# Causal attention on one core: softmax sums by rounded ones, clips in the bank, other order of roundings

## What is computed

```python
x = L0_attn_x                                  # (4, 512, 512), float32
xn = _layernorm(x)
x = x + _L0_attn_ref(xn, ...) + _L0_ffn_ref(xn, ...)

def _L0_attn_ref(x, W_DQ, W_UQ, W_QR, W_DKV, W_UK, W_UV, W_KR, W_O):   # 16 heads of 128, rotary part of 64
    c_Q = x @ W_DQ.T                                                   # latent of 128
    q = concat([c_Q @ W_UQ.T, rope(c_Q @ W_QR.T)])                     # per head
    c_KV = x @ W_DKV.T
    k = concat([c_KV @ W_UK.T, rope(x @ W_KR.T)])                      # rotary part shared by all heads
    v = c_KV @ W_UV.T
    scores = clip(einsum('bhqd,bhkd->bhqk', q, k), -80, 80)
    scores = where(causal, scores, -inf)
    weights = softmax(scores / sqrt(192))
    return (weights @ v, heads side by side) @ W_O.T
```

## Time and profile before

| | |
|---|---|
| median of 3 runs | 1333.8 us (1333.33 to 1334.8) |
| profiled execution | 1334.99 us, its span 1333.0 us |
| PE busy | 1304.3 us, 98% |
| DVE busy | 736.7 us, 55% |
| ACT busy | 620.4 us, 47% |
| POOL busy | 627.9 us, 47% |
| in 900 to 1000 us | PE 100.0, DVE 84.8, ACT 65.5, POOL 69.6 us |
| mean granted clock of PE | 0.996 |

### The profile page before, as it was taken

One profiled execution on the slowest core, in us unless ns is written; L12 is line 12 of the kernel. 1 busy time (PEld: TensorE's weight loads), 2 busy tenths in 40 slices (PEclk: granted clock), 3 DMA queues, 4 the chain that ended last, 5 costly groups with the idle time before them and its releaser, 6 DMA issues.

```text
span 1333.0 us, 21124 instructions
## 1 busy us (share of the span) xinstructions
PE 1304.3 (98%) x6553; PEld 1090.8 (82%) x6553; DVE 736.7 (55%) x1349; ACT 620.4 (47%) x1146; POOL 627.9 (47%) x534
## 2 busy tenths in 40 slices
PE   5999999999999999999997999999999999999999
PEld 4788888888888888888885888888888888888887
DVE  6361154332222222222224878988888888788876
ACT  6421243222222222222224766676667666766674
POOL 5125584994060005000003467666766676666543
PEclk9999999999999999999998999999999999999999
DMA  8225453664142114212115123233233332322012
GB/s 268 65 87 220 185 187 96 186 187 143 57 151 64 57 57 127 86 57 64 57 52 181 34 47 70 65 64 74 39 83 63 61 64 58 77 43 60 17 48 95
DMA packets 72952, 123.23 MB, mean 92 GB/s; under 512 B 10960, under 2 KB 19280, under 8 KB 72848
## 3 DMA queue, kind: packets, MB, share of 16 engines
q1 hardware_dynamic: 42000, 60.49, 15.8%
q0 software_dynamic: 11312, 27.23, 9.5%
q10 hardware_dynamic: 19536, 34.17, 7.7%
HBM read 74.41 MB, written 39.05 MB: 85 GB/s over the span
## 4 chain that ended last, share of the span: by engine, by line
PE 94%; DVE 2%; DMA 1%; SPq 1%; POOL 1%; issue 1%; ACT 0%; ACTq 0%; DVEq 0%; POOLq 0%
PE bank L48 83%; PE bank L1676 4%; PE bank L1461 2%; PE bank L1403 2%; PE bank L1546 1%; SPq L442 1%; DMA rows_b<-in_x 1%; DMA raw<-in_wot 0%; PE bank L1389 0%; POOL slots L484 0%; DVE stats L905 0%; DVE store_b L1291 0%; SPq L428 0%; PE bank L1522 0%; DVE acc L1318 0%
## 5 line engine op out<-in xcount | busy, mean ns | idle before, releaser
L48 PE MATMUL bank<-store_b,store_a 128*128 128x512 f32 (+1 forms) x1536 | 322.8, 363 | 2.2 <-DVE store_b L1217 1.9
L48 PE MATMUL bank<-slots,x_turned 128*128 x1296 | 317.6, 394 | 0.3 <-DVE x_turned L929 0.3
L48 PEld LDWEIGHTS bank<-store_b,store_a 128*128 128x128 f32 x1536 | 255.4, 190 | 54.1 <-issue 9.0
L48 PEld LDWEIGHTS bank<-slots,x_turned 128*128 128x128 f32 x1296 | 239.3, 188 | 48.1 <-issue 0.5
L951 DVE TENSOR_TENSOR hid_t<-bank,hid_t 128x512 fp32r<-128x512 f32 x70 | 48.3, 691 | 343.6 <-ACT hid_t L668 343.6
L48 PE MATMUL bank<-slots,hid_t 128*128 (+1 forms) x840 | 208.4, 397 | 0.0
L48 PE MATMUL bank<-store_b 128*128 128x512 f32 x768 | 179.4, 389 | 0.0
L48 PEld LDWEIGHTS bank<-slots,hid_t 128*128 128x128 f32 x840 | 153.7, 188 | 31.1 <-DVE hid_t L951 0.3
L48 PEld LDWEIGHTS bank<-store_b 128*128 128x128 f32 x768 | 144.1, 188 | 29.9
L842 ACT ACTIVATE p_store<-bank 128x512 f32<-128x512 f32 x160 | 95.6, 597 | 86.2 <-PE bank L48 84.6
L538 POOL CAST slots<-staging 128x512 f32 (+1 forms) x84 | 51.7, 615 | 171.7 <-PE bank L48 169.5
(11 more groups left out here) (203 smaller groups left out, 1820.9 us busy)
## 6 DMA issues: line engine op xcount, KB each, us to landing
staging<-in_w SPq DMA_DIRECT2D x56, 256.0 KB, 2.8
sorted_y<-y_store ACTq DMA_DIRECT2D x54, 256.0 KB, 2.0
rows<-sorted_x ACTq DMA_DIRECT2D x51, 260.0 KB, 2.7
rot_sin<-sum_b SPq DMA_DIRECT2D x128, 64.0 KB, 2.0
staging<-in_wg SPq DMA_DIRECT2D x28, 256.0 KB, 2.8
shared_y<-y_store ACTq DMA_DIRECT2D x16, 256.0 KB, 2.4
raw<-in_wot SPq DMA_DIRECT2D x16, 256.0 KB, 2.9
acc<-in_x SPq DMA_DIRECT2D x16, 256.0 KB, 5.6
```

What stands on the lines that cost most here:

```text
L48: made = pe.matmul(out, a, b, start=first and n == 0, stop=last and n == len(pairs) - 1, skip_group_check=onto)
```

## The change

1. **Sums.** Before, eight matmuls with the float32 probabilities as stationary operand and a column of ones, 16 passes. Now `unit_r`, a rounded pair of columns (of ones and zeros) that picks the row it sums into, is stationary, and the high and low parts of group 0, of the first half of group 2 and of `sum_b` are moved through it, into two rows of the bank. `sum_a` goes; `sum_b` is rounded into `sum_b_hi` (ACT) and `sum_b_lo` (POOL). The two rows are copied by ACT (`divisor_rows`), and two DMAs turn them into columns (`sum_store`), from which `invert` works.
2. **Clips.** DVE now clips the scores while it takes them from the bank, and the exponential is made of the clipped scores in place. The bank is free after the clip.
3. **Rotary.** The cosine product reads the bank itself. `rotate_high` has two ACT copies in place of three, `krot` low is kept for all 128 rows, and its zeroing on POOL goes.
4. **Order.** The roundings of the next queries move from the middle of a unit to behind the outputs of the unit before (DVE) and behind `round_high(u, 4)` (ACT). `invert` moves behind the clips; on DVE clips 3 and 4 stand ahead of the low parts.
5. **Loads.** The raw weights of pair 1 are issued ahead of the 16 loads of `acc`, not after unit 1's swap.

```diff
@@ tiles and ring
+        sum_b_hi, sum_b_lo = (carve(2 * H2, "down").rearrange("p (h t) -> p h t", h=2) for _ in range(2))
-        one = tile(ctx, "one", [P, 8])
+        unit = tile(ctx, "unit", [P, 2, 2])
+        unit_r = tile(ctx, "unit_r", [P, 2, 2], F32R)
+        sum_store = tile(ctx, "sum_store", [P, 2, 2, 2, 2])
...
             elif kind == "scores":
-                pe.wait_ge(on["exps_done"], NG * n[0] + n[1] + 1)
+                pe.wait_ge(on["clipped"], NG * n[0] + n[1] + 1)
...
             elif kind == "sums":
-                pe.wait_ge(on["ratio_made"], n[0] + 1)
+                pe.wait_ge(on["rows_made"], n[0] + 1)
@@ SP
             swap_halves(0)
+            for h in heads_of(0):
+                head_weights(1, h)
             sp.wait_ge(on["y_done"], NBK)
...
-                for h in heads_of(u):
+                for h in heads_of(u) if u else ():
                     head_weights(p + 1, h)
+                sp.wait_ge(on["rows_made"], u + 1)
+                if u >= 2:
+                    sp.wait_ge(on["ratio_made"], u - 1)
+                for s in range(2):
+                    sp.dma_start(sum_store[:, u % 2, s].rearrange("p h t -> p (h t)"),
+                                 divisor_rows[s:s + 1, :].rearrange("o (p c) -> o p c", p=P)).then_inc(
+                        on[f"divisor_sent{u % 2}"], 16)
@@ POOL
-                pool.wait_ge(on["clipped"], NG * u + 3)
-                pool.tensor_tensor(sum_a[:], w[0][:, :, P:2 * P], w1_q1, ALU.add).then_inc(on["sum_step"], 1)
                 if u + 1 < NU:
                     sine(u + 1)
...
                 if u + 1 < NU:
                     rotate(u + 1)
+                pool.wait_ge(on["sums_high"], u + 1)
+                pool.tensor_tensor(sum_b_lo, sum_b[:], sum_b_hi.bitcast(F32), ALU.subtract).then_inc(
+                    on["sums_low"], 1)
@@ ACT
             def exponents(u, g):
-                act.wait_ge(on["scores_done"], NG * u + g + 1)
-                prob_slot_free(act, u, g)
-                act.activation(prob(u, g), ring.bank("scores", u, g), ACT.Exp, scale=SCALE).then_inc(
-                    on["exps_done"], 1)
+                act.wait_ge(on["clipped"], NG * u + g + 1)
+                act.activation(prob(u, g), prob(u, g), ACT.Exp, scale=SCALE).then_inc(on["exps_done"], 1)
...
                 act.activation(qr[up, 0, :], rot[up, :], ACT.Copy)
-                act.activation(qr[dn, 1, :], rot[dn, :], ACT.Copy)
-                act.activation(qr[up, 1, :], rot[dn, :], ACT.Copy).then_inc(on["qr_high"], 1)
+                act.activation(qr[dn, 1, :], rot[dn, :], ACT.Copy).then_inc(on["qr_high"], 1)
...
                 round_high(u, 2)
-                if u + 1 < NU:
-                    query(u + 1, 0)
-                    query(u + 1, 1)
...
                 round_high(u, 4)
+                if u + 1 < NU:
+                    query(u + 1, 0)
+                    query(u + 1, 1)
+                act.wait_ge(on["sum_step"], 3 * u + 3)
+                act.activation(sum_b_hi, sum_b[:], ACT.Copy).then_inc(on["sums_high"], 1)
...
+                act.wait_ge(on["dens_done"], u + 1)
...
+                act.activation(divisor_rows[:].rearrange("s (p c) -> s c p", p=P),
+                               ring.bank("sums", u)[0:2, :].rearrange("s (c p) -> s c p", p=P), ACT.Copy).then_inc(
+                    on["rows_made"], 1)
@@ DVE
-                dve.tensor_tensor(rot[:], rot_raw, cos_t[:], ALU.mult).then_inc(on["cosine_done"], 1)
+                dve.tensor_tensor(rot[:], ring.bank("rotate", u), cos_t[:], ALU.mult).then_inc(on["cosine_done"], 1)
...
-                dve.wait_ge(on["exps_done"], NG * u + g + 1)
-                w = prob(u, g)
+                dve.wait_ge(on["scores_done"], NG * u + g + 1)
+                prob_slot_free(dve, u, g)
+                w, bank = prob(u, g), ring.bank("scores", u, g)
                 if g in (1, 3):
-                    made = dve.tensor_scalar(w, w, low, high, ALU.max, ALU.min)
+                    made = dve.tensor_scalar(w, bank, -CLIP, CLIP, ALU.max, ALU.min)
...
-                if u:
-                    invert(u - 1)
                 clip(u, 0)
                 clip(u, 1)
+                clip(u, 2)
                 if u + 1 < NU:
                     rotate(u + 1)
-                clip(u, 2)
-                take_low(u, 1)
                 clip(u, 3)
                 clip(u, 4)
+                if u:
+                    invert(u - 1)
+                take_low(u, 1)
                 take_low(u, 2)
-                if u + 1 < NU:
-                    query(u + 1, 0)
-                    query(u + 1, 1)
                 take_low(u, 3)
...
                 if u:
                     output(u - 1, 2)
                     output(u - 1, 3)
+                if u + 1 < NU:
+                    query(u + 1, 0)
+                    query(u + 1, 1)
                 if u + 1 < NU:
                     rotate_low(u + 1)
@@ PE
-                    for h in range(2):
-                        w = (first[:, h, 0:P], sum_a[:, h, :], sum_b[:, h, 0:P], sum_b[:, h, P:2 * P])[tt]
-                        n = 4 * (tt // 2) + 2 * h + tt % 2
-                        made = pe.matmul(ring.bank("sums", u)[:, n:n + 1], w, one[:, 0:1], start=True, stop=True)
-                made.then_inc(on["dens_done"], 1)
+                product(pe, row, [(unit_r[:, 0, :], s[0]) for s in (p_hi, p_lo)], last=False)
+                product(pe, second_half, [(unit_r[:, 0, :], s[2][:, 0:2 * P].rearrange("p (h t) -> p h t", h=2))
+                                          for s in (p_hi, p_lo)], first=False, last=False)
+                pe.wait_ge(on["sums_low"], u + 1)
+                product(pe, row.rearrange("p (h t) -> p h t", h=2),
+                        [(unit_r[:, 1, :], sum_b_hi), (unit_r[:, 1, :], sum_b_lo)], first=False).then_inc(
+                    on["dens_done"], 1)
```

More of the change, by code:

```diff
@@ L22 @@
 CLIP = 80.0
+LATER = -30000.0
 class Turns:
@@ L260, in program @@
              "q_done", "q_high", "q_low", "scores_done", "exps_done", "clipped", "p_high", "p_low0", "p_low",
-             "sum_step", "o_done", "o_high", "o_low", "dens_done", "inverted",
+             "sum_step", "o_done", "o_high", "o_low", "sums_high", "sums_low", "dens_done", "rows_made", "inverted",
              "ratio_made", "part_done", "rescaled", "out_done", "out_added")
@@ L333, in ring_bank_free @@
                 pe.wait_ge(on["rot_copied"], n[0] + 1)
+                pe.wait_ge(on["cosine_done"], n[0] + 1)
             elif kind == "head":
@@ L556, in pool_program @@
             pool.wait_ge(on["scale_made"], NR)
-            pool.memset(cap[:], float(np.exp(CLIP * SCALE))).then_inc(on["cap_filled"], 1)
+            pool.memset(cap[:], CLIP).then_inc(on["cap_filled"], 1)
             pool.wait_ge(on["cap_filled"], 1)
-            pool.affine_select(out=cap[:, 0:P], in_=cap[:, 0:P], compare_op=ALU.is_ge, fill=0.0, base=0,
+            pool.affine_select(out=cap[:, 0:P], in_=cap[:, 0:P], compare_op=ALU.is_ge, fill=LATER, base=0,
                                pattern=[[1, P]], channel_multiplier=-1).then_inc(on["cap_made"], 1)
-            pool.memset(one[:], 1.0).then_inc(on["one_made"], 1)
+            pool.memset(unit[:], 0.0).then_inc(on["unit_made"], 1)
+            pool.wait_ge(on["unit_made"], 1)
+            for s in range(2):
+                pool.memset(unit[:, s, s:s + 1], 1.0).then_inc(on["unit_made"], 1)
             def sine(u):
@@ L851, in rescale @@
                     on["rescaled"], 1)
+            act.wait_ge(on["unit_made"], 3)
+            act.activation(unit_r[:], unit[:], ACT.Copy).then_inc(on["unit_rounded"], 1)
             head_weights(0, 0, 0)
@@ L973, in turn @@
                 dve.tensor_tensor(cq[:, 1, cols], bank[:, P:2 * P], cq[:, 0, cols].bitcast(F32), ALU.subtract)
-                dve.tensor_tensor(krot[0:DR, 1, cols], bank[0:DR, 2 * P:3 * P], krot[0:DR, 0, cols].bitcast(F32),
+                dve.tensor_tensor(krot[:, 1, cols], bank[:, 2 * P:3 * P], krot[:, 0, cols].bitcast(F32),
                                   ALU.subtract).then_inc(on["lat_low"], 1)
@@ L1302, in clip @@
                     n = P if g == 2 else 2 * P
-                    part = w.rearrange("p (h t) -> p h t", t=n)
-                    made = dve.scalar_tensor_tensor(part, part, low, cap[:, 0:n].unsqueeze(1).broadcast_to(
+                    part, scored = (v.rearrange("p (h t) -> p h t", t=n) for v in (w, bank))
+                    made = dve.scalar_tensor_tensor(part, scored, -CLIP, cap[:, 0:n].unsqueeze(1).broadcast_to(
                         [P, BANK // n, n]), ALU.max, ALU.min)
@@ L1322, in invert @@
             def invert(u):
-                sums = ring.bank("sums", u)[:, 0:8].rearrange("p (n h t) -> p n h t", n=2, h=2)
-                dve.wait_ge(on["dens_done"], u + 1)
-                dve.reciprocal(inv_store[:, u % 2], sums).then_inc(on["inverted"], 1)
```

(21 more changed lines are left out.)

55 lines of the change are left out of this document (25 added, 30 removed).

## The result

The changed kernel takes 1367.44 us (median of 4, 1366.73 to 1369.01) against 1333.76 us: ratio 1.0254, 95% interval 1.0242 to 1.0266, slower by 34 us. The forecast was 1392 us, range 1362 to 1410. The profiled execution has a span of 1367.2 us (1333.0 before). Lines are those of the changed kernel from here on.

A forecast was written before the change was run, and what follows sets the result against it. PE, busy 98% of the span, was taken as the bound. Head units +60, unit 0 -0.7, units without a head -5, MoE additions +1, tail +3.4 sum to +58.7: 1392 us against the median, range 1362 to 1410.

The forecast's parts named there:

- Sums: PE's sum matmuls in each unit: 1.16 us in place of 1.80, 0.6 us saved, 0.4 at worst.
- The wait: PE's head matmuls wait for DVE's moved query rounding, from 13.13 to about 16.8: 3.7 us per head unit, floor 2.1.
- The clock: PE runs at the lower clock for about 4 us behind each head wait: 2.0 us lost, 1.6 at least.
- the MoE additions: DVE additions ahead of the clips that now precede the exponentials, in the rotary loop: +1 us in all.
- Units without a head: 18 units bounded by the rotary loop go from 18.55 to 18.2 to 18.3 us: -5 us, bounds -11 and +5.
- The loads: Unit 0: the raw weights' wait goes, but PE then waits for sum_b_lo: -0.7 us, bounds -8.6 and +1.
- The tail: Last output: PE waits 2.0 us for the rescale, up to 2 of clock, less the sums' 0.6: +3.4, bounds 0 and +6.
- Clips: DVE's clips from the bank take 0.6 to 0.7 us each and make POOL wait less in the rotary loop: -0.3.
- Rival (a): PE's clock holds over the 3.7 us head waits: +31, 1365 us; chance 0.10.
- Rival (d): PE's head wait stays at its floor of 2.1 us with 1.6 of clock behind it: 1369 us; chance 0.09.
- (b): Rotary loop or sum_b_lo is later, 0.5 to 1 us in each of 18 units: about 1406 us; chance 0.14.
- (c): The head's bank is not late, DVE rounds the queries before PE asks; only savings remain: 1325 us; chance 0.05.

The follow-up runs named there:

- experiment 1: Changed kernel with the two query roundings back in their old places on ACT and DVE: 1322.64 us, ratio 0.9914 to the kernel before.
- experiment 2: Changed kernel with PE's head matmuls moved behind attend and their ring turns behind the sums: 1327.07 us, ratio 0.9946 to the kernel before.
- experiment 3: Kernel before with only the two query roundings moved, behind round_high 4 on ACT and output 3 on DVE: 1396.87 us, ratio 1.0475.
- experiment 5: Changed kernel with 12 extra, unused PE matmuls before the head matmuls in each of 12 head units: 1355.31 us, ratio 1.0155 to the kernel before.
- Experiment 8: Changed kernel with query roundings back, only four acc loads ahead of unit 1's swap, ACT's rotary copy ahead of group 1's exponential: 1311.96 us, ratio 0.9828.
- experiment 6: Changed kernel with pair 1's raw weights loaded as before, behind the acc loads and unit 1's swap: 1367.89 us, ratio 1.0255 to the kernel before.
- experiment 9: Changed kernel with query roundings back and clips again on the exponentials in SBUF: 1320.29 us, ratio 0.9888 to the kernel before.

## Why the prediction was right, and where its sizes were off

The direction and its cause stand: the moved query rounding makes the head's bank late, 12 times, and nothing else in the change loses time on that scale (experiments 1, 2 and 3). By the steps:

- **Sums.** Forecast 1.16 us, measured 1.05: 0.75 us saved a unit, not 0.6.
- **The wait.** Forecast 13.13 to 16.8, 3.7 us; measured 13.23 to 16.11, 2.9 us by the loads (2.49 by the matmul records, 2.56 on average of the 12). DVE's queue ran as worked out up to the outputs 0 and 1: clips to 7.59 (7.45), sine at 8.62 (8.46), take_low 2 to 10.47 (10.4), take_low 3 to 12.16 (12.2), outputs to 13.48 (13.6). The step that failed is take_low 4: I put it behind POOL's third sum, to 14.7. In the trace both start at 928.28, and it is DVE's that takes its plain 0.68 (to 14.08), while POOL's half-width sum stretches to 1.27 (0.72 where it meets nobody). It is not one unit's chance: in 26 of the 32 units the two start within 16 ns of each other, DVE takes 0.68 and POOL 1.26 to 1.29. From there all is 0.7 sooner. The Trainium skill, "SBUF — State Buffer", section "SBUF: two separate sides", says that an operation of DVE with two inputs in SBUF and one of GpSimd exclude each other for the whole instruction, and whichever starts first has the ports; the trace agrees that one of the two runs in its plain 0.68 while the other takes 1.27, but it can't show who was first: by its records POOL starts 6 ns ahead of DVE here.
- **The clock.** Forecast 2.0 us behind each wait, measured 1.1 (experiment 5). The sentence that failed is that a wait between 1.9 and 6.6 us would be followed by the lower level each time. It was in 8 of 12, at 1.9 us on average. The head units as a whole, 12 x (5.0 - 3.65), are 16 of the 25 us by which the forecast was too high. The other 9 are the units without a head (4.5), the tail (1.6), the start with unit 0 (1.3), and 1 us for the MoE additions, which the table does not hold apart.
- **Units without a head.** Forecast 18.2 to 18.3, measured 18.06: -9.5 in place of -5. The loop is there (17 waits for line 1227, 5.0 us, in the changed kernel), but it binds less than I worked out. Experiment 8 shows its link: the copy on ACT.
- **The loads.** Forecast -0.7 for unit 0 and what is late next, `sum_b_lo` at 733.8 with the weights' wait gone. Measured: its matmul at 732.67, 8.33 us of wait. Unit 0 itself gave +1.0, and the start ahead of it -2.95, which I had not forecast: the first scores came 1.4 us sooner and ran at full level (2.55 us for ten matmuls, 4.12 before). That the earlier load is worth nothing is shown (experiment 6).
- **The tail.** Forecast 2.0 of wait, 2 of clock, 3.4 in all; measured 2.30, no fall of the clock, 1.8 in all. The ACT copy took 1.06 where I had 0.6. The path of the last ratios, DVE and PE:

```profile
1359.64 0.20 DVE L1346 RECIPROCAL inv_store<-sum_store 128x8 f32<-128x8 f32 x1 [3.50 <-DMA sum_store<-divisor_rows]
...
1360.94 3.02 PE L49 MATMUL bank<-store_b 128*128 128x512 f32 x12 [2.30 <-ACT bank L861]
```

- **Clips.** I took 0.6 to 0.7, measured 0.685, and counted them as a gain for the loop. With the queries in place no gain is shown: experiment 9 is 0.3% on the other side, with overlapping intervals.

Two rivals are nearer to the time than the forecast, for sizes that happen to add. Rival (a), the clock holds, was right in a third of the waits, and its 1365 has a wait of 3.7 us in it. Rival (d), 1369, is the nearest, with 3.1 us a head unit against 3.65; but the wait did not stay at its floor of 2.1, it was 2.9. Rivals (b) and (c) fall: units without a head became shorter, and the wait was there.

Experiment 3's head units (24.50) are longer than the changed kernel's (23.26) by 0.5 us more than the sums explain, with an average wait about the same (2.64). The clock can carry that: it fell at 12 waits there, at 8 here, and four falls of 1.9 us over 12 units are 0.6.

Open: what decides, at equal length of a wait, whether the clock falls, and so why it fell each time in experiment 3.

## What to carry to other kernels

When banks go round in a ring, read from the ring which result frees each one, and let that result stand in its engine's queue ahead of anything that the waiting engine has yet to produce. A step off the path with 1.7 us to spare cost 62 us when it was put behind six others, the last of which needs what PE has only just made. Undo one part of a change at a time: here the order alone lost more than the whole change did, the rest was worth 0.9% and with two small steps 1.7%, and two improvements of the same loop did not add.

## What the runs showed of the hardware that I had not expected

- A pause of PE of 2.49 us left the granted clock at full level, one of 2.47 us was followed by 0.50, and one of 1.77 us by full level where 1.89 us had been followed by 0.59. On average 12 pauses of 2.1 to 3.1 us cost 1.1 us of clock each (experiment 5). In experiment 3 pauses of 2.27 us were followed by 0.50 as well, while in the changed kernel one of 2.56 was not.
- PE ran 144 more matmuls in 12 us less, since they kept it busy in the pauses.
- A two-column weight takes PE no load time worth counting: six matmuls of 512 or 256 columns from such weights took 1.05 us, 2560 columns at 2.4 GHz being 1.07.
- Where a DVE subtraction with both inputs in SBUF and POOL's half-width sum start together, DVE took its plain 0.68 us and POOL 1.27 in place of 0.72, in 26 of 32 units.
- An ACT copy of 2 by 512 from a bank, written with a stride of 16 bytes, took 1.06 us (line 916), where 128 by 512 takes 0.60; and two DMAs that turn rows into columns landed 2.6 us after the first was issued (1357.00 to 1359.64 with DVE's start).
